# A new written order for all five engines of a two-layer transformer kernel, with GpSimd's hold on VectorE's port counted

## The reference, cut to what matters

```python
# stage A, x: (8, 1024, 256), one head of 64, causal over 1024 tokens
q, k, v = x @ wq + bq, x @ wk + bk, x @ wv + bv
x = layernorm(x + softmax(q @ k.T / 8 + causal_mask) @ v @ wo + bo)

# stage B, two layers on the same (8, 1024, 256)
h = shift_token(x)                    # second half of the channels comes from the token before
q, k, v = split(h @ wqkv)             # 8 heads of 64
q, k = rotary_xpos(l2norm(q) * qs, l2norm(k) * ks)
x1 = x + local_attention(8 * q, k, v) @ wo   # windows of 128, looking one window back, softmax
h = layernorm(shift_token(x1)) * g + b
a, u = split(h @ w1 + b1)             # 682 columns each
x2 = x1 + (a * gelu(u)) @ w2 + b2

# at the end
out = layernorm(x + x2_of_layer_1)    # x: the result of stage A
```

## Time and profile before

| what | us |
|---|---|
| median of 3 runs | 2688.95 |
| lowest and highest | 2684.12, 2690.76 |
| span of the profiled execution | 2682.5 |
| PE busy | 2626.4 (98%) |
| PEld busy | 2309.2 (86%) |
| DVE busy | 2276.5 (85%) |
| ACT busy | 1934.8 (72%) |
| POOL busy | 1658.1 (62%) |

### The profile page before, as it was taken

How to read it: one execution, slowest core, us unless ns; L and a number is a source line. 1 busy time by engine, 2 the same in 40 slices (tenths; PEclk the granted TensorE clock), 3 DMA queues, 4 the chain that set the end, 5 groups by cost and what they waited for, 6 DMA issues and landing times.

```text
span 2682.5 us, 65519 instructions
## 1 busy us (share of the span) xinstructions
PE 2626.4 (98%) x22240; PEld 2309.2 (86%) x22240; DVE 2276.5 (85%) x6866; ACT 1934.8 (72%) x4826; POOL 1658.1 (62%) x1753
## 2 busy tenths in 40 slices
PE   8999999999999999999999999999999999999998
PEld 5677688899998899998999898989988999988887
DVE  5778988888888888888888889898989989998786
ACT  5655588777777777777777777777777777778775
POOL 6523755566566556666665676666766667766563
PEclk9999999999999999999999999999999999999999
DMA  9931300000001100000001211011101111111110
GB/s 314 334 105 59 107 21 24 29 24 29 27 27 55 44 25 29 25 29 24 28 25 60 93 31 36 30 37 33 37 30 34 33 33 37 31 36 34 30 32 23
DMA packets 144510, 140.37 MB, mean 52 GB/s; under 512 B 16024, under 2 KB 126128, under 8 KB 143408
## 3 DMA queue, kind: packets, MB, share of 16 engines
q1 hardware_dynamic: 144176, 136.18, 16.0%
HBM read 80.02 MB, written 51.92 MB: 49 GB/s over the span
## 4 chain that ended last, share of the span: by engine, by line
PE 61%; DVE 2%; ACT 1%; issue 1%; DMA 1%; SPq 0%; POOL 0%; DVEq 0%; ACTq 0%; POOLq 0%
PE p_pair L173 13%; PE p_pair L174 10%; PE p_pair L175 10%; PE p_values L2551 6%; PE p_turn L2540 5%; PE p_mixed L173 4%; PE p_mixed L175 4%; PE p_mixed L174 4%; PE p_turn L2522 2%; PE p_turn L2516 1%; PE p_mixed L2486 1%; PE p_mixed L2568 1%; PE p_mixed L2594 0%; PE p_mixed L2593 0%; ACT prob L1224 0%
## 5 line engine op out<-in xcount | busy, mean ns | idle before, releaser
L960 POOL TENSOR_TENSOR prob<-prob,rinv 128x512 f32<-128x512 f32 (+1 forms) x512 | 506.5, 1001 | 393.0 <-DVE rinv L1771 392.7
L1224 ACT ACTIVATE prob<-prob,least 128x256 f32<-128x256 f32 (+1 forms) x1024 | 496.2, 487 | 63.2 <-DVE least L1763 61.7
L938 POOL TENSOR_TENSOR inv_norm<-norm_clipped,minus_half 128x8 f32<-128x8 f32 x256 | 423.0, 1659 | 79.2 <-DVE norm_clipped L1727 71.8
L1763 DVE CUSTOM_DVE_ANT_0 prob<-p_pair,mask,inv_norm 128x256 f32<-128x256 f32 (+1 forms) x1024 | 440.2, 460 | 35.0 <-PE p_pair L175 33.0
L173 PE MATMUL p_pair<-hT_h,w_h 128*128 128x256 f32 (+1 forms) x1408 | 410.1, 291 | 6.9 <-ACT v L1218 2.5
L174 PE MATMUL p_pair<-hT_l,w_h 128*128 128x256 f32 (+1 forms) x1408 | 391.1, 278 | 0.0
L175 PE MATMUL p_pair<-hT_h,w_l 128*128 128x256 f32 (+1 forms) x1408 | 391.0, 278 | 0.0
L1236 ACT ACTIVATE pT<-p_turn 128x512 f32<-128x512 f32 (+1 forms) x512 | 283.7, 569 | 76.3 <-PE p_turn L2540 63.9
L173 PEld LDWEIGHTS p_pair<-hT_h,w_h 128*128 128x128 f32 (+1 forms) x1408 | 262.6, 186 | 22.7 <-issue 10.8
L1835 DVE SCALAR_TENSOR_TENSOR gated<-p_pair,columns,gelu 128x256 f32<-128x256 f32 (+1 forms) x384 | 184.0, 481 | 108.5 <-ACT gelu L1263 106.4
L2540 PE MATMUL p_turn<-ident,prob 128*128 128x128 f32 x1920 | 266.5, 273 | 0.8 <-POOL prob L960 0.5
(11 more groups left out here) (147 smaller groups left out, 7970.3 us busy)
## 6 DMA issues: line engine op xcount, KB each, us to landing
x_tile<-x_rows SPq DMA_DIRECT2D x192, 128.0 KB, 2.1
a_wraw<-in_w_all SPq DMA_DIRECT2D x32, 264.0 KB, 5.3
w_high<-a_wraw_h SPq DMA_DIRECT2D x32, 264.0 KB, 3.9
w_low<-a_wraw_l SPq DMA_DIRECT2D x32, 264.0 KB, 4.7
a_x<-in_x SPq DMA_DIRECT2D x32, 256.0 KB, 4.2
x_rows<-a_x SPq DMA_DIRECT2D x64, 128.0 KB, 1.8
x_tile<-x_rows SPq DMA_DIRECT2D x128, 64.0 KB, 2.0
mid_rows<-x_mid SPq DMA_DIRECT2D x128, 64.0 KB, 1.7
```

Source lines behind the costliest of these rows:

```text
L938: pool.tensor_tensor(r[:, t.slot(2), heads], rt[:, heads], half[:, heads], ALU.pow).then_inc(pool_r[n], 1)
L960: pool.tensor_tensor(p, p, rinv[:, 2 * m:2 * m + 2].unsqueeze(2).to_broadcast([P, 2, cols.stop - cols.start]), ALU.mult).then_inc(pool_p, 1)
L1224: act.activation(prob[:, h, cols], prob[:, h, cols], ACT.Exp, bias=least[:, h:h + 1], scale=-1.0, accum_out=rsum[:, h:h + 1]).then_inc(act ...
L1763: dve.tensor_tensor_reduce(prob[:, h, cols], p_score[h % 2][:, c0 + cols.start:c0 + cols.stop], mask[:, a.slot(2), cols], r[:, a.slot(2), ...
```

## The change

All five lists are drawn anew: `first_on_...`, `step` and `last_steps`. The loop now runs from step 12 (before: from 8 on SP and GpSimd, 9 on ScalarE and VectorE, 11 on PE) to 59, as before. All operations on data are the same ones with the same buffers and sizes (calls that do nothing for a tile of layer 0 stand in the new lists in other places); the orders and the `after` waits differ. What of PE's and VectorE's step matters most, without the `after` lines that stay:

```diff
 # PE, step
 turn_probs(T(6), 3)
 project_v(T(4))
-turn_probs(T(5), 0)
 turn_x(T(3))
-scores(T(5), 1)
 values(T(6), 0) ... values(T(6), 3)
-project_k(T(3), 0)
-project_k(T(3), 1)
-turn_h(Q(4))
-turn_q(T(4))
-turn_probs(T(5), 1)
-project_q(T(3))
+scores(T(5), 1)
+project_q(T(3))
+project_k(T(3), 0)
+turn_h(Q(4))
+turn_probs(T(5), 0)
+turn_probs(T(5), 1)
+project_k(T(3), 1)
+turn_q(T(4))
 turn_k(T(4))
+after((dve_hv, Q(4), 1, 1))
 output(T(6))
 project_v(T(3))
 turn_probs(T(5), 2)
 turn_probs(T(5), 3)
 scores(T(4), 0)
 values(T(5), 0) ... values(T(5), 3)
+after((dve_least, T(4), H, 4))
+scores(T(4), 1)
 widen(Q(4), 0)
 widen(Q(4), 1)
-scores(T(4), 1)
+widen(Q(4), 2)
+widen(Q(4), 3)
 turn_k(T(3))
+turn_q(T(3))
 output(T(5))
-widen(Q(4), 2)
-widen(Q(4), 3)
-turn_q(T(3))
 widen(Q(4), 4)
 turn_x(T(2))
 widen(Q(4), 5)
 turn_probs(T(4), 0)
 turn_probs(T(4), 1)
 scores(T(3), 0)
 project_k(T(2), 0)
 project_k(T(2), 1)
 narrow(T(8))
 project_q(T(2))
 narrow(T(7))
 turn_probs(T(4), 2)
```

VectorE's step before and after, first half:

```diff
-norms(T(4), 1); rope_sin(T(4), 0, 0); final(T(10)); final(T(9)); rope_sin(T(4), 0, 1); clip(T(4), 1); x_low(T(3)); q_sum(T(4))
-least_of(T(5), 4); least_of(T(5), 5); norms(T(4), 0); least_of(T(5), 6); least_of(T(5), 7)
-o_low(T(6)); norms(T(3), 1); h_affine(Q(4)); rope_cos(T(3), 1); clip(T(3), 1); inverse_sums(T(5), 1)
-rope_sin(T(3), 1, 0); rope_sin(T(3), 1, 1); k_low(T(4)); q_low(T(4)); clip(T(4), 0); rope_cos(T(3), 0); middle(T(6))
-rope_sin(T(3), 0, 0); h_low(Q(4)); rope_sin(T(3), 0, 1); least_of(T(4), 0) ... least_of(T(4), 3)
+rope_sin(T(4), 0, 1); final_statistics(T(9)); x_low(T(3)); norms(T(4), 1)
+least_of(T(5), 4); clip(T(4), 1); least_of(T(5), 5); least_of(T(5), 6); least_of(T(5), 7); q_sum(T(4)); final(T(10)); norms(T(4), 0)
+o_low(T(6)); h_affine(Q(4)); inverse_sums(T(5), 1); clip(T(4), 0); rope_cos(T(3), 1)
+rope_sin(T(3), 1, 0); rope_sin(T(3), 1, 1); k_low(T(4)); q_low(T(4)); rope_cos(T(3), 0)
+rope_sin(T(3), 0, 0); rope_sin(T(3), 0, 1); norms(T(3), 0); norms(T(3), 1); least_of(T(4), 0) ... least_of(T(4), 3)
```

In the second half both `statistics` stand behind `gated_low(Q(4), 5)` (before: `statistics(T(6))` among the `least_of` of `T(4)`). GpSimd's `k_sum(T(2))` moved ahead of `normalise(T(3), 0)`, and `final_inverse_std` and `residual_x1` serve other tiles (`T(9)` and `T(8)`, `T(7)` and `T(6)`, instead of `T(8)` and `T(7)` each). On SP:

```diff
 store_mid(T(6))
-load_shifted(T(6))
-load_x1(T(8))
 store_mid(T(5))
+load_shifted(T(6))
 load_shifted(T(5))
-load_x(T(1))
-load_x(T(0))
+load_x(T(2))
+load_x(T(1))
```

(`load_x` of the even tile now stands ahead of `store_mid(T(6))`.) In `last_steps`, PE's list before breaks `values` up and puts other work between, as in this cut, and ends with `narrow(T(125))` behind `turn_h(Q(126))`; after, it keeps the order of the loop to about tile 125:

```diff
 # PE, last_steps, a cut
-turn_probs(T(117), 2); scores(T(118), 0); turn_probs(T(117), 3); values(T(117), 2); turn_q(T(119)); widen(Q(114), 0); scores(T(118), 1); values(T(117), 3)
+turn_probs(T(117), 2); turn_probs(T(117), 3); scores(T(118), 0); values(T(117), 0) ... values(T(117), 3); scores(T(118), 1); widen(Q(114), 0)
...
-output(T(127)); widen(Q(124), 2) ... widen(Q(124), 5); turn_h(Q(126)); narrow(T(124)); widen(Q(126), 0); widen(Q(126), 1); narrow(T(125)); widen(Q(126), 2) ...
+widen(Q(124), 2); widen(Q(124), 3); output(T(127)); widen(Q(124), 4); widen(Q(124), 5); narrow(T(124)); narrow(T(125)); turn_h(Q(126)); widen(Q(126), 0) ...
```

More of the change, by code:

```diff
@@ L2066, in last_steps @@
             least_of(T(118), 3)
-            statistics(T(116))
-            inverse_sums(T(118), 0)
+            h_low(Q(114))
+            q_sum(T(119))
+            final(T(113))
             least_of(T(118), 4)
@@ new lines, in first_on_vector @@
+    t.clip(T(14), 0)
+    t.inverse_sums(T(13), 1)
+    t.o_low(T(12))
+    t.h_affine(Q(10))
+    t.rope_cos(T(15), 1)
+    t.rope_sin(T(15), 1, 0)
+    t.rope_sin(T(15), 1, 1)
+    t.k_low(T(14))
+    t.q_low(T(14))
+    t.norms(T(15), 1)
+    t.rope_cos(T(15), 0)
+    t.rope_sin(T(15), 0, 0)
+    t.rope_sin(T(15), 0, 1)
+    t.clip(T(15), 1)
+    t.h_low(Q(10))
+    t.least_of(T(14), 0)
+    t.least_of(T(14), 1)
+    t.least_of(T(14), 2)
+    t.least_of(T(14), 3)
+    t.o_low(T(13))
+    t.gated(Q(10), 0)
@@ new lines, in first_on_vector @@
+    t.gated(Q(10), 1)
+    t.q_sum(T(15))
+    t.least_of(T(14), 4)
+    t.least_of(T(14), 5)
+    t.norms(T(15), 0)
+    t.final(T(9))
+    t.middle(T(12))
+    t.clip(T(15), 0)
+    t.gated_low(Q(10), 0)
+    t.gated(Q(10), 2)
+    t.gated(Q(10), 3)
+    t.gated_low(Q(10), 1)
+    t.gated_low(Q(10), 2)
+    t.gated_low(Q(10), 3)
+    t.inverse_sums(T(14), 0)
+    t.middle(T(13))
+    t.q_low(T(15))
+    t.k_low(T(15))
+    t.least_of(T(14), 6)
+    t.least_of(T(14), 7)
+    t.gated(Q(10), 4)
@@ new lines, in first_on_vector @@
+    t.rope_sin(T(17), 1, 1)
+    t.k_low(T(16))
+    t.q_low(T(16))
+    t.rope_cos(T(17), 0)
+    t.rope_sin(T(17), 0, 0)
+    t.rope_sin(T(17), 0, 1)
+    t.norms(T(17), 0)
+    t.middle(T(14))
+    t.least_of(T(16), 0)
+    t.clip(T(17), 0)
+    t.least_of(T(16), 1)
+    t.least_of(T(16), 2)
+    t.least_of(T(16), 3)
+    t.norms(T(17), 1)
+    t.h_low(Q(12))
+    t.q_sum(T(17))
+    t.inverse_sums(T(16), 0)
+    t.least_of(T(16), 4)
+    t.least_of(T(16), 5)
+    t.least_of(T(16), 6)
+    t.o_low(T(15))
@@ new lines, in first_on_vector @@
+    t.clip(T(17), 1)
+    t.gated(Q(12), 0)
+    t.gated(Q(12), 1)
+    t.gated(Q(12), 2)
+    t.gated_low(Q(12), 0)
+    t.middle(T(15))
+    t.k_low(T(17))
+    t.q_low(T(17))
+    t.least_of(T(16), 7)
+    t.gated(Q(12), 3)
+    t.gated_low(Q(12), 1)
+    t.gated_low(Q(12), 2)
+    t.x_low(T(18))
+    t.gated(Q(12), 4)
+    t.gated(Q(12), 5)
+    t.gated_low(Q(12), 3)
+    t.gated_low(Q(12), 4)
+    t.gated_low(Q(12), 5)
+    t.least_of(T(17), 0)
+    t.least_of(T(17), 1)
+    t.least_of(T(17), 2)
@@ new lines, in first_on_vector @@
+    t.rope_sin(T(19), 0, 0)
+    t.rope_sin(T(19), 0, 1)
+    t.norms(T(19), 0)
+    t.norms(T(19), 1)
+    t.least_of(T(18), 0)
+    t.least_of(T(18), 1)
+    t.least_of(T(18), 2)
+    t.least_of(T(18), 3)
+    t.clip(T(19), 1)
+    t.h_low(Q(14))
+    t.final(T(13))
+    t.middle(T(16))
+    t.least_of(T(18), 4)
+    t.least_of(T(18), 5)
+    t.gated(Q(14), 0)
+    t.inverse_sums(T(18), 0)
+    t.clip(T(19), 0)
+    t.gated(Q(14), 1)
+    t.q_sum(T(19))
+    t.o_low(T(17))
+    t.gated_low(Q(14), 0)
```

5293 lines of the change are left out of this document (2777 added, 2516 removed).

## The result

The changed kernel takes 2657.54 us (median of 4 runs, 2653.78 to 2663.11) against 2686.53 for the kernel before, run beside it (2683.65 to 2690.76): ratio 0.9891, 95% interval 0.9874 to 0.9908, so 29.0 us less by the medians. Forecast were 2671 and a range from 2658 to 2690. The profiled spans are 2655.9 and 2682.5 us, 26.6 apart where 18.0 were forecast.

The account below looks back on a forecast made before the run. TensorE's own work was taken as the bound, busy 1837.15 of 1840 us in the middle. Terms 7.2 + 6.7 + 4 + 3 - 2.4 - 0.5 = 18.0 took the span to 2664.5, the median to 2671; range 2658 to 2690.

Parts of the forecast that it names:

- The start: First part, before the loop: shape changes fall from 272 to 223, priced 6.5 us, 4 kept since waits can swallow part.
- R2: Rival, 2660 us: start loses nothing, layer 1 adds no wait, 5 to 8 us of end idle go; chance 0.16.
- Place (a): Loop: `output(T(6))` waits for `h_affine(Q(4))`; margin 0.3 us in layer 0, 0 in layer 1.
- R3: Rival, slower, 2698 us: `q_sum(T(4))` meets `k_scaled` or the power, VectorE's row 0.6 us late 48 times; chance 0.14.
- The loop's toll: TensorE's loop: array shape changes fall from 10 to 9 a step, saving 0.15 us a step, 7.2 over 48 steps.
- The signs that the prediction named: Right: middle step 36.9 us, TensorE above 99.5% busy, `q_rot` (`q_sum`) 0.68 nearly everywhere; wrong: `hT` waits over 5 us.
- R4: Rival: `q_rot` keeps running into `k_sum`, 1.62 us long; time as forecast within 2 us; shares the forecast's chance, 0.52.
- The up to 0.9 us a step that I let VectorE win: Loop, VectorE: `q_sum` behind `least_of(T(5), 7)` avoids GpSimd's `k_sum`, 0.68 us instead of 1.62; worth nothing in the middle.
- Place (b): Loop: earlier `scores(T(4), 1)` waits for `least_of(T(4), 3)`, which meets TensorE within 0.1 us either way.
- The ends: Last steps: shape changes fall from 110 to 60, saving 6.7 us, plus 3 of 7.6 us idle in 2400:2640.
- The tail: Kernel's end: `narrow(T(125))` ahead of `turn_h(Q(126))` covers one wait but opens about 2.7 us; value 0, bounds -2 and +2.
- SP's queue: On SP `load_shifted(T(6))` waits behind `store_mid(T(5))`; late transfers cost 0.5 us in all, ends 0 and 3.

Follow-up runs that it names:

- the second two profiles: Both kernels run once more unchanged, one execution each, for a second profile: kernel before 2681.05 us, changed kernel 2660.14 us.
- the swap: Against the changed kernel, `final(T(10))` stands ahead of `q_sum(T(4))` in VectorE's step instead of behind it: 2638.03 us, ratio 0.9823 to the kernel before.
- the split of `values(T(6))`: Against the changed kernel, `values(T(6), 0)` moved ahead of `project_v(T(4))` and `turn_x(T(3))` in TensorE's step: 2675.3 us, ratio 0.9959 to the kernel before.

## Why the prediction was wrong where it was

**The start (4 us forecast, 20 to 23 measured): the step that failed by most.** I priced only the changes of shape there, 6.5, and struck off a third because a wait can swallow them. By the four rows up to pair 8, mean of the two profiles of each kernel, the 21.7 us between them are: 4.8 less idle (34.0 and 29.3), 9.0 less for the clock (TensorE is busy at 1.2 GHz for 28.2 and 10.2 us, and half of the difference is lost time; the distances between matmuls there, held against those at full clock, give 9.2), and 7.9 left over, which for the 51 changes of shape fewer in the records (287 and 236) is 0.15 each, with nothing swallowed.

So the largest part of all was a term that the sum put at nothing. It was named only in rival R2, with 5 to 8 us of idle for both ends and no figure for the clock. The rows had one: a granted clock of 0.98 over 560 us is 22 us at half speed (27.3 by the trace), 11 us or more of lost time, which I read and did not price. The runs show that the new order has less idle and less half clock together, and each of the stretches at half clock behind a gap; that the smaller idle is the cause of the better clock they don't show, and I tried nothing that would.

**Place (a), 2.4 forecast, some 20 lost.** Right: the place, the waiting call, its position in layer 1, and the margin (layer 0 shows no such wait, layer 1 one in nearly every step). Wrong: the size, 0.80 a step for the 0.1 taken, above the 0.6 a step of the bounds, though its total lies inside their 29 us because only the 24 steps of layer 1 pay. The wait isn't new either: the list before has `after((dve_hv, Q(4), 1, 1))` ahead of `output(T(6))` too; what changed is how far apart the two stand. I counted `final` at 0.41, its length before, and moved it to 0.08 us ahead of a `k_scaled` without asking whom it meets there; against R3 I had written that `k_scaled` starts when `q_sum` is half through, but it starts when `q_sum` ends, which is when the next operation begins. I had asked this of `q_sum`, with two inputs in SBUF; `final` has one and is held as well. R3 had this mechanism and nearly this price (0.6) but the wrong victim, and charged it in all 48 steps.

"SBUF — State Buffer" of the Trainium skill, section "SBUF: two separate sides", says that an operation of VectorE in a two-port performance mode takes the lock too, not only one with two SBUF inputs; whether `final` runs in such a mode no row says, but that it is held at all (1.27 against 0.41) agrees with the rule. Two things in the trace stand against it. The rule gives the ports to whichever starts first, and by the records `final` starts 0.03 to 0.08 ahead of `k_scaled` in all 23 cases and is the one held; GpSimd's times are rough in the profile, and the start of a record need not be the moment at which the ports are asked for. And the power, which the same rule counts, holds neither `q_sum` (0.68) nor `final` (0.41).

**The loop's toll, 7.2 forecast.** The records show 10 changes of shape a step before and 9 after, and a plain step of layer 0 went from 37.15 to 36.99: the toll is right. In layer 0, from pair 8 to 32, 6.6 us came of 24 steps where 3.6 were due (4.8 in the second two profiles). Of them 3.4 come from three long steps of the kernel before (38.13, 36.13 and 38.21 for pairs 13 to 15, with 0.2 to 0.7 us of idle in each) that fell to the common length; the other steps with which a batch begins gained 0.22. With (a) out of the way, pair 8 to 56 takes 1756.1 us against 1769.1: the new loop is worth 12.9 and not 7.2. Waits of the old order are part of the rest, 2.9 us idle in the middle against 0.4 from pair 8 to 56 with the swap; some 3 us are left open.

The signs that the prediction named came out mixed: 37.0 a step in layer 0 but 37.9 in layer 1, TensorE busy 99.2% of the middle and not over 99.5, `q_sum` short in half of its cases and not nearly everywhere, a wait on `hT` of 14.6 us where over 5 was to mean R3. So R4 came true in kind, with `residual` in the place of `k_sum`. The up to 0.9 us a step that I let VectorE win rested on taking `q_sum(T(4))` for the held one; what it won is 0.14 a step, and in the sum this stood at nothing for the middle.

**Place (b).** Within 0.1 either way was right: no wait for `least_of` is listed in the middle of the changed kernel, and one of up to 0.8 stands in nearly every step as soon as half of `values` no longer covers it.

**The ends (6.7 + 3 = 9.7 forecast, 9.5 measured).** Right in the sum and not in its parts, which is luck. From pair 56 on TensorE is idle 18.4 and 18.9 us before and 17.3 and 17.4 after, so of the idle part 1.3 came and not 3. It is busy at half clock for 6.8 and 0 us before and for 11.4 and 6.3 after, which costs the new end 2.7. So about 11 us are left for 50 changes fewer, 0.22 each where 0.13 was forecast and no split measured more than 0.17 on one side; that is what remains, not a measurement, and what else is in it is open. The tail was about nothing, as taken: `hT_l` 2.5 for `h_norm` and `hT` 2.7.

**SP's queue (0.5).** No wait of TensorE traces back to it; below what can be seen.

**From the span to the time.** I added 6.4 us, the distance of the profiled span to the median of the runs. Executions lie only 1.6 to 1.8 over their own spans (2684.12 and 2682.5; 2657.68 and 2655.9); the rest was that this execution was a quick one. So 8.6 of the 13.5 us by which 2671 missed are the span's, most of the rest this.

In all: start 21.7, loop without (a) 12.9, (a) -20, ends 9.5, together 24, near the 23.8 between the mean spans of two profiles each. 18.0 had come from terms of which one was a fifth and one an eighth of its true size, with opposite signs: errors of 18 us for the start, 6 for the loop and 18 the other way for (a). That the sum came within 6 us of the measured one is luck.

## What to carry to other kernels

When a written order is judged by who holds whom, check every operation that lands in the dangerous place, not only the one that was moved for it: swapping two neighbours (`final`, `q_sum`) was worth 19 us, as much as two thirds of the whole redesign. Price a granted clock below 1.00 in a stretch as its own term (here it was worth 9 us), and take a second profile before believing where half-speed stretches lie. A test that adds a toll must leave the distance between producers and consumers alone, or it measures a wait.

## What the runs showed of the hardware that I had not expected

- A VectorE `TENSOR_SCALAR` of 128x256 from SBUF to SBUF takes 0.41 us beside GpSimd's 128x8 power and 1.27 beside its 128x512 multiply, although its record starts first. One of 128x128 for `normed` takes 0.33 to 0.35 in half of the cases and 0.54 to 1.08 in the half beside `normalise`.
- Entering another array shape costs 0.17 us behind transposes (the split of `values(T(6))`) and about 0.10 behind other matmuls. "TensorEngine Tiling (Array Packing)" of the Trainium skill, section "Key Properties", says that such a switch needs a drain and gives no time for it; these are the times here.
- In rows of 128x256 matmuls of the changed kernel without a wait the distance is either 113 or 118 ns at a granted clock of 1.00, for a whole row at a time: 0.2 us on 48 of them. The kernel before has 113 or 114.
- One execution ran at a granted clock of 0.948 from 12 us to its end and was 10 to 15 us longer than its neighbours of the same kernel (2653.78 against 2638.72, 2639.08 and 2644.12).
